# First layer of a three-layer attention kernel: the order of VectorE's work inside a softmax step, and who makes half of a low part

## The chip, the cores and the metric

One core of one Trainium2 chip. The metric is the device time of one launch, in microseconds (us). Engines as the profile names them: PE is TensorE, DVE is VectorE, ACT is ScalarE, POOL is GpSimd, SP is SyncE, which only issues the loads and stores here.

## The reference, cut to what matters

Sixteen sequences of 128 tokens, width 512. A grouped-query cross-attention layer (32 query heads of width 16, 8 key heads), a residual and a layer norm with scale and offset; then two cross-attention layers (16 heads of width 128, one extra key and value each) with a pre-norm, and an MLP of 2048. The change touches the first layer only:

```python
q = (x @ Wq + bq);  k = (ctx @ Wk + bk);  v = (ctx @ Wv + bv)      # per head
s = q @ k.T / 4 + mask
p = softmax(s)                       # max, exp, sum, reciprocal, product
o = (p @ v) @ Wo + bo + x
y = layernorm(o) * gamma + beta      # eps 1e-6
```

## The kernel before, in words

**Numbers in two parts.** Matrix operands of the projections are kept as a rounded part ("high") and the rest ("low", the value less its high part), and each product is three matrix products over them (`PASSES`, line 25). So every projected tile is evicted from PSUM twice: ScalarE writes the high part, then VectorE computes value less high part from the same PSUM bank. `qlo0` (line 1462) does so for the queries, `cxlo0` (line 1490) for the contexts, `klo0` (line 1453) for the keys. The four source tensors (`src_hi`, `src_lo`, numbers 0 to 3) get their high part from ScalarE (`high`, line 1146) and their low part from VectorE (`low`, line 1431) or GpSimd (`low`, line 448).

**Two halves.** The outer loop `hf` runs over two halves of eight sequences. In each, the first layer is 32 softmax steps (`STEPS0`); a step `s` is one sequence and eight heads. Four steps make a unit, and every unit has a projected query tile and gives a context tile. Every fourth to eighth step carries extra work: a query projection at the steps of `Q_AT` (line 45), an output product `out0` at those of `ROWS_AT` (line 52), a piece of a later weight split or an add of the output bias on GpSimd at those of `SPLIT_AT` and `BO_AT`.

**A step, engine by engine.** Each engine runs its own list in the order written, and waits on semaphores.

- TensorE, step `s` (line 834): transposes `t0(s)` (needs `norm0` of GpSimd), product with the values `pv0(s-1)`, scores `s0_(s+4)` (line 729; needs `z0` of the step before, since there is one set of score banks, and `q0_lo`), a query projection if `s` is in `Q_AT`, an output product `out0(s)` (line 770) if it is in `ROWS_AT`.
- VectorE, step `s` (line 1591): `rec0(s+1)` (a sum over three heads and a reciprocal), `cxlo0` if due, `qlo0` if due, `soft0(s+3)`, and the row work `add0` if due: it adds the output product to the residual `X` (line 1440).
- `soft0(s)` (line 1468) is two instructions: the masked copy (line 1473) reads the scores from PSUM, adds the mask, writes them to SBUF and raises `z0`; the maximum (line 1478) reads that copy, after a wait on `z0`, and raises `max0`.
- ScalarE, step `s` (line 1239): copies the transposes out of PSUM, evicts the high part of a query or context tile, then does the exponentials of step `s+3` (five heads with the maximum as bias, three heads after GpSimd's subtraction).
- GpSimd, step `s` (line 531): `norm(s+1)` (the product with the reciprocals, line 479), `sub(s+3)` (subtracts the maximum from three heads, line 472; needs `max0`), then the bias add or weight pieces.

**One bank, three users.** The query projection and `out0` write the same PSUM bank, `BA`. So `out0` waits for the low part of the last query that was projected there, and the next writer waits for the row work (`xadd`):

```python
def out0(s):                                                   # line 770
    pe.wait_ge(cx0_lo, u0 + (2 * n + 2))
    pe.wait_ge(q0_lo, u0 + 2 + sum(k < s for k in Q_AT))
    if n or t:
        pe.wait_ge(xadd, x0 + (n * BT + t))
```

`Q_AT` has the steps 0, 3, 8, 12, 16, 20, so `qlo0` runs on VectorE at steps 2, 5, 10, 14, 18, 22. `ROWS_AT` has 9, 10, 11, 13, 17, 18, 19, 21, 25, 26, 27, 28, so `add0` runs at 10, 11, 12, 14, 18, 19, 20, 22, 26, 27, 28, 29. Both fall on steps 10, 14, 18 and 22. `cxlo0` runs at steps 5, 9, 13, 17, 21, 25 and 29.

**The start of the first half.** VectorE makes both parts (two instructions) of the low part of source 3 between `soft0(2)` and the steps, line 1589. GpSimd's list there is `sub(0)`, `sub(1)`, `norm(0)`, `sub(2)` (line 527). In the second half that low part is made elsewhere (line 1575).

Of the kernel before, what the change touches and what calls it, by code (L numbers as in the profile page):

```python
# [17 lines left out]
F32 = mybir.dt.float32  # L18
F32R = mybir.dt.float32r
ALU = mybir.AluOpType  # L20
# [9 lines left out]
SEQ = 8  # L30
TB = 2
BT = SEQ // TB
# [12 lines left out]
Q_AT = {0: 2, 3: 3, 8: 4, 12: 5, 16: 6, 20: 7}  # L45
# [6 lines left out]
ROWS_AT = {9: (0, 0), 10: (0, 1), 11: (0, 2), 13: (0, 3), 17: (1, 0), 18: (1, 1), 19: (1, 2), 21: (1, 3),  # L52
           25: (2, 0), 26: (2, 1), 27: (2, 2), 28: (2, 3)}
# [24 lines left out]
def build(nc, x, xT, cT, mask, wq, wk0, wk, wv0, wv, wo, vec, ident_in, gb_rows, bo_rows, bv_rows, biasv_rows, out):  # L78
    ctx = ExitStack()
    with ctx:  # L80
# [3 lines left out]
        def sem(name):  # L84
            return ctx.enter_context(nc.semaphore(name))

        X = sb("X", [P, SEQ, D])
        at = (nc.sbuf_base + 31) // 32 * 32
# [29 lines left out]
        at = (nc.sbuf_base + 127) // 128 * 128  # L118
# [43 lines left out]
        BA, BB, BC, BD, BS, BPT, BPV = 0, 1, 2, 3, 4, 6, 7  # L162
# [15 lines left out]
        src_hi, src_lo = [sem(f"{k}_hi") for k in ("c0", "x0", "c1", "x1")], [sem(f"{k}_lo") for k in ("c0", "x0", "c1", "x1")]  # L178
# [15 lines left out]
        bo_tile, bo_added, vb_done, low_rows = sem("bo_tile"), sem("bo_added"), sem("vb_done"), sem("low_rows")  # L194
# [15 lines left out]
        def source(i, p, a):  # L210

            return (CT, AT)[i % 2][:, a, 2 * p:2 * p + 2, i // 2 * BTOK:(i // 2 + 1) * BTOK]

        def raw_source(i, p):

            return RAWS[i % 2][:, 1, 2 * p:2 * p + 2, i // 2 * BTOK:(i // 2 + 1) * BTOK]
# [10 lines left out]
        def jj0(u):  # L227

            return u // 4 * 2 + u % 2

        def tile0(s):

            return s // 8 % 2 * BT + s % 4
# [192 lines left out]
        def _(pool):  # L426
# [38 lines left out]
            for hf in range(HALVES):  # L465
                nq, nv = hf * Q_SLABS, hf * V_SLABS

                def sub(s):

                    pool.wait_ge(max0, hf * STEPS0 + (s + 1))  # L470
                    z = P0[s % BUFS0].rearrange("p (h t) -> p h t", t=P)[:, OWN:KV0, :]
                    nc.gpsimd.tensor_tensor(z, z, MX[:, s % BUFS0, OWN:KV0].unsqueeze(2).to_broadcast([P, KV0 - OWN, P]),  # L472
                                            ALU.add).then_inc(sub0, 1)

                def norm(s):

                    pool.wait_ge(rc0, hf * STEPS0 + (s + 1))
                    z = P0[s % BUFS0].rearrange("p (h t) -> p h t", t=P)
                    nc.gpsimd.tensor_tensor(z, z, RC[:, s % 2, :].unsqueeze(2).to_broadcast([P, KV0, P]),  # L479
                                            ALU.mult).then_inc(norm0, 1)  # L480
# [44 lines left out]
                    nc.gpsimd.tensor_tensor(BVR[:, 0:256], BVR[:, 0:256], ROWV[:, 0:256], ALU.subtract).then_inc(vb_done, 1)  # L525

                sub(0)
                sub(1)
                norm(0)
                sub(2)  # L530
                for s in range(STEPS0):
# [8 lines left out]
                    if s in SPLIT_AT:  # L540
                        n, parts = SPLIT_AT[s]
# [17 lines left out]
                for ly in range(LAYERS):  # L559
# [53 lines left out]
                    n = b0 + (NB1 - 1)  # L613
# [804 lines left out]
        def _(dve):  # L1418
            V_ = nc.vector
# [11 lines left out]
            def low(hf, i):  # L1431

                for p in range(2):
                    dve.wait_ge(src_hi[i], hf * 2 + (p + 1))
                    V_.tensor_tensor(source(i, p, 1), raw_source(i, p), source(i, p, 0).bitcast(F32),  # L1435
                                     ALU.subtract).then_inc(src_lo[i], 1)

            def add_rows(bank, tile, filled, count, done):
                dve.wait_ge(filled, count)
                V_.tensor_tensor(X[:, tile, :], PS[:, bank, :], X[:, tile, :], ALU.add).then_inc(done, 1)  # L1440
# [8 lines left out]
            for hf in range(HALVES):  # L1449
# [3 lines left out]
                def klo0(tb):  # L1453
                    dve.wait_ge(k0_hi, hf * TB + (tb + 1))
                    for e in range(2):
                        tiles = slice(tb * BT, (tb + 1) * BT)
                        ins = V_.scalar_tensor_tensor(KZ[:, 1, tiles, e, :], KF[:, tb, :].rearrange("p (b t) -> p b t", t=P),
                                                      VEC[:, COL_EVEN + e:COL_EVEN + e + 1], KZ[:, 0, tiles, e, :].bitcast(F32),
                                                      ALU.mult, ALU.subtract)
                    ins.then_inc(k0_lo, 1)  # L1460

                def qlo0(u):
                    jj = jj0(u)
                    dve.wait_ge(q0_hi, u0 + (u + 1))
                    V_.scalar_tensor_tensor(Q0[:, u % 2, 1, :], PS[:, BA, :], VEC[:, COL_BQ0 + jj:COL_BQ0 + jj + 1],  # L1465
                                            Q0[:, u % 2, 0, :].bitcast(F32), ALU.add, ALU.subtract).then_inc(q0_lo, 1)

                def soft0(s):
                    tile = tile0(s)
                    dve.wait_ge(s0_ps, s0 + (s + 1))  # L1470
                    if s >= BUFS0:
                        dve.wait_ge(t0_ps, s0 + (s - BUFS0 + 1))
                    V_.tensor_tensor(P0[s % BUFS0].rearrange("p (i e t) -> p i e t", e=2, t=P),
                                     PS[:, B0:B0 + 4, 0:256].rearrange("p i (e t) -> p i e t", t=P),
                                     BIASVR[:, tile * P:(tile + 1) * P].unsqueeze(1).unsqueeze(1).to_broadcast([P, 4, 2, P]),
                                     ALU.add).then_inc(z0, 1)
                    dve.wait_ge(z0, s0 + (s + 1))
                    V_.tensor_reduce(MX[:, s % BUFS0, :], P0[s % BUFS0].rearrange("p (h t) -> p h t", t=P),
                                     AXX, ALU.max, negate=True).then_inc(max0, 1)

                def rec0(s):
                    dve.wait_ge(exp0, s0 + (s + 1))
                    V_.tensor_reduce(SUM0[:, s % 2, OWN:KV0], P0[s % BUFS0].rearrange("p (h t) -> p h t", t=P)[:, OWN:KV0, :],
                                     AXX, ALU.add).then_inc(sum0, 1)
                    if s >= 2:
                        dve.wait_ge(norm0, s0 + (s - 1))
                    dve.wait_ge(sum0, s0 + (s + 1))
                    V_.reciprocal(RC[:, s % 2, :], SUM0[:, s % 2, :]).then_inc(rc0, 1)

                def cxlo0(u):  # L1490
                    dve.wait_ge(cx0_hi, u0 + (u + 1))
                    V_.scalar_tensor_tensor(CX0[:, u % 3, 1, :], PS[:, BB, :], VEC[:, COL_BV0:COL_BV0 + 1],
                                            CX0[:, u % 3, 0, :].bitcast(F32), ALU.add, ALU.subtract).then_inc(cx0_lo, 1)

                def add0(n, t, bank):
                    add_rows(bank, n % 2 * BT + t, o0_ps, o0 + (n * BT + t + 1), xadd)

                def stats(tb, tiles, added):

                    for i, b in enumerate(tiles):
                        dve.wait_ge(xadd, added + i)
                        V_.bn_stats(BNS[:, b, :], X[:, tb * BT + b, :]).then_inc(ln_stats, 1)
# [5 lines left out]
                def variances(r, eps):  # L1509

                    dve.wait_ge(ln_stats, r * BT + BT)
                    take_wait(dve)
                    for b in range(BT):
                        ins = V_.bn_aggr(MV[:, b, :], BNS[:, b, :])
                    step(r, 1, ins)
                    V_.tensor_scalar(NT[:], MV[:, :, 1], eps, -0.5, ALU.add, ALU.mult).then_inc(ln_step, 1)
# [63 lines left out]
                if hf:  # L1580
                    last_down((0, 1))
                qlo0(1)
                soft0(1)
                rec0(0)
                if hf:
                    last_down((2, 3))
                soft0(2)
                if hf == 0:
                    low(0, 3)
                x0 = hf * (ROWS0 + LAYERS * NB1 * BT)  # L1590
                for s in range(STEPS0):
                    if s + 1 < STEPS0:
                        rec0(s + 1)
                    if s % 4 == 1 and s > 1:
                        cxlo0(s // 4 - 1)
                    if s - 2 in Q_AT:
                        qlo0(Q_AT[s - 2])
                    if s + 3 < STEPS0:
                        soft0(s + 3)
                    if s == 0:  # L1600
                        klo0(1)
                    if s - 1 in ROWS_AT:
                        n, t = ROWS_AT[s - 1]
                        if n < 2:
                            dve.wait_ge(bo_tile, hf * SEQ + (n * BT + t + 1))
                        add0(n, t, BA)
                    if s == 29:
                        stats(0, range(BT), x0 + 9)
                        variances(hf * 8, 1e-6)
                    if s == 30:  # L1610
                        roots(hf * 8)
                        own(0, 0)
# [322 lines left out]
```

## Time and profile before

| | us |
|---|---|
| median of three runs (2405.12, 2407.29, 2408.05) | 2407.29 |
| the profiled execution, its own time | 2409.09 |
| its span, first to last instruction | 2407.0 |
| PE busy | 2347.7 |
| DVE busy | 1209.7 |
| ACT busy | 871.2 |
| POOL busy | 813.7 |

How to read it: the span is what the trace shows; the own time is 2.09 us more, which lies outside it. PE is busy almost throughout, but the first layer of each half is a short stage in which the four engines hand small tiles to one another, and the averages over the whole say little of it. Steps 0 to 31 of the first half lie between 33 us and 165 us of the span, those of the second half between 1227 us and 1360 us. In a row of the timeline the columns are: start, duration, engine, line, operation, what is written and read, shapes, count, and in brackets the idle time of that engine before it and who ended it. Idle of less than 0.15 us gets no brackets. MX is written by the maximum, XN, HF and P0D are the four buffers of masked scores (XN holds two), CX, Q and X are written by the context, query and row work.

### The profile page before, as it was taken

What the parts mean: (1) busy time and instruction counts of PE and PEld (TensorE: products, weight loads), DVE (VectorE), ACT (ScalarE), POOL (GpSimd) and SP (SyncE); (2) the same over time, 40 slices, a digit from 0 to 9 for tenths busy, and PEclk for the clock granted to TensorE, in tenths of its full rate; (3) what the DMA queues carried; (4) which work ended last, traced back from release to release, by engine and by line L of the source; (5) the groups of instructions that cost most, each with busy time, mean ns of one, the idle gap of its engine ahead of it and who ended that gap; (6) DMA issues with size and microseconds to landing.
All of it is one profiled execution on the core that took longest, in us unless ns stands there. A gap on an engine that the chain in (4) does not pass through costs nothing.

```text
span 2407.0 us, 35909 instructions
## 1 busy us (share of the span) xinstructions
PE 2347.7 (98%) x13616; PEld 1967.9 (82%) x13616; DVE 1209.7 (50%) x2037; ACT 871.2 (36%) x2511; POOL 813.7 (34%) x599
## 2 busy tenths in 40 slices
PE   7999999999999999999989999999999999999999
PEld 5677888888888888878867778888888888888887
DVE  6985333344533334465679843343354333344655
ACT  7964222232422222342378642222233222134311
POOL 6974323233422323120059543231343323132100
PEclk9999999999999999999999999999999999999999
DMA  5002111111101111211320021110111111110110
GB/s 207 12 19 84 36 36 52 44 62 58 36 25 46 35 44 44 66 44 62 112 86 11 19 83 36 44 61 27 62 58 36 36 36 35 44 53 14 62 44 35
DMA packets 37845, 120.54 MB, mean 50 GB/s; under 512 B 3664, under 2 KB 3920, under 8 KB 37712
## 3 DMA queue, kind: packets, MB, share of 16 engines
q1 hardware_dynamic: 37712, 118.69, 14.6%
q8 instruction: 93, 1.52, 0.3%
q14 instruction: 40, 0.33, 0.0%
HBM read 114.48 MB, written 4.19 MB: 49 GB/s over the span
## 4 chain that ended last, share of the span: by engine, by line
PE 85%; POOL 7%; DVE 4%; ACT 2%; issue 2%; DMA 0%; SPq 0%; POOLq 0%; DVEq 0%; ACTq 0%
PE PS L652 72%; PE PS L880 5%; PE PS L896 4%; PE PS L888 2%; POOL XN L479 1%; DVE X L1440 1%; POOL XN L472 1%; POOL W L503 1%; POOL HF L479 1%; ACT AT L1266 1%; POOL P0D L479 1%; POOL X L513 1%; ACT PS L1266 1%; POOL W L428 1%; PE PS L752 0%
## 5 line engine op out<-in xcount | busy, mean ns | idle before, releaser
L652 PE MATMUL PS<-AT,W 128*128 128x512 f32 x2496 | 605.4, 393 | 8.7 <-DVE AT L1561 5.4
L652 PEld LDWEIGHTS PS<-AT,W 128*128 128x128 f32 x2496 | 467.7, 189 | 113.8 <-DVE AT L1561 11.7
L1440 DVE TENSOR_TENSOR X<-PS,X 128x512 f32<-128x512 f32 x416 | 286.0, 689 | 359.4 <-PE PS L652 353.6
L550 POOL TENSOR_TENSOR PR<-PR,RC 128x512 f32<-128x512 f32 x128 | 133.4, 1042 | 926.4 <-DVE RC L1649 926.4
L652 PE MATMUL PS<-W,CX 128*128 128x512 f32 x1632 | 403.8, 398 | 6.9 <-DVE Q L1465 4.6
L652 PE MATMUL PS<-CT,W 128*128 128x512 f32 x1584 | 394.1, 398 | 7.7 <-DVE CT L1435 7.7
L652 PE MATMUL PS<-WV,CT 128*128 128x512 f32 (+1 forms) x1920 | 367.1, 349 | 0.0
L652 PEld LDWEIGHTS PS<-W,CX 128*128 128x128 f32 x1632 | 298.0, 188 | 72.5 <-issue 7.1
L652 PEld LDWEIGHTS PS<-WV,CT 128*128 128x128 f32 x1920 | 308.7, 189 | 45.5 <-issue 0.8
L652 PEld LDWEIGHTS PS<-CT,W 128*128 128x128 f32 x1584 | 289.5, 189 | 62.4 <-issue 7.9
L1293 ACT ACTIVATE CX<-PS,VEC 128x512 fp32r<-128x512 f32 x128 | 88.3, 690 | 648.2 <-PE PS L896 648.2
L1282 ACT ACTIVATE PR<-PS,MX 128x129 f32<-128x129 f32 x512 | 182.2, 370 | 177.5 <-DVE MX L1643 177.5
L1276 ACT ACTIVATE Q<-PS,BQS 128x512 f32<-128x512 f32 x128 | 88.2, 689 | 327.4 <-PE PS L652 327.4
L1688 DVE TENSOR_TENSOR VV<-PS,BVR 128x512 f32<-128x512 f32 x96 | 66.4, 692 | 258.4 <-PE PS L652 258.4
L428 POOL TENSOR_SCALAR W<-RAW 128x1024 fp32r<-128x1024 f32 (+2 forms) x107 | 96.2, 899 | 262.5 <-PE PS L652 214.2
L421 POOL TENSOR_TENSOR W<-RAW,W 128x1024 fp32r<-128x1024 f32 (+1 forms) x67 | 159.7, 2383 | 5.6
L1680 DVE SCALAR_TENSOR_TENSOR CX<-PS,VEC,CX 128x512 fp32r<-128x512 f32 x128 | 96.1, 751 | 129.2 <-ACT CX L1293 129.2
L880 PE MATMUL PS<-K,Q 128*128 128x129 f32 x1024 | 135.8, 276 | 0.9 <-ACT Q L1276 0.9
L1394 ACT ACTIVATE HF<-PS,VEC 128x512 f32<-128x512 f32 x64 | 44.0, 688 | 239.7 <-PE PS L652 239.7
L880 PEld LDWEIGHTS PS<-K,Q 128*128 128x128 f32 x1024 | 124.6, 192 | 1.6 <-ACT Q L1276 1.3
L1649 DVE RECIPROCAL RC<-SUM 128x4 f32<-128x4 f32 x128 | 22.7, 178 | 194.2 <-ACT PR L1282 194.2
L896 PEld LDWEIGHTS PS<-PT,VV 128*128 128x128 f32 x768 | 100.5, 191 | 7.5
(124 smaller groups left out, 2910.1 us busy)
## 6 DMA issues: line engine op xcount, KB each, us to landing
RAW<-in_wq SPq DMA_DIRECT2D x44, 512.0 KB, 4.3
RAW<-in_wo SPq DMA_DIRECT2D x44, 512.0 KB, 3.5
RAW<-in_wk SPq DMA_DIRECT2D x40, 512.0 KB, 3.5
RAW<-in_wv SPq DMA_DIRECT2D x40, 512.0 KB, 3.9
raw_c<-in_cT SPq DMA_DIRECT2D x8, 512.0 KB, 6.9
raw_x<-in_xT SPq DMA_DIRECT2D x8, 512.0 KB, 6.0
BVR<-in_bv_rows SPq DMA_DIRECT2D x8, 512.0 KB, 3.6
X<-in_x SPq DMA_DIRECT2D x4, 1024.0 KB, 10.8
```

The lines of the kernel that those rows point to most:

```text
L421: eng.tensor_tensor(SLAB[n][:, 1, 0:width], RAW[:, n, 0:width], SLAB[n][:, 0, 0:width].bitcast(F32), ALU.subtract).then_inc(w_ready[n], 1)
L428: return nc.gpsimd.tensor_scalar(out, in_, 1.0, 0.0, ALU.mult, ALU.add)
L479: nc.gpsimd.tensor_tensor(z, z, RC[:, s % 2, :].unsqueeze(2).to_broadcast([P, KV0, P]), ALU.mult).then_inc(norm0, 1)
L550: nc.gpsimd.tensor_tensor(PR[:, :, 0:P], PR[:, :, 0:P], RC[:, 0, 0:BT].unsqueeze(2).to_broadcast([P, BT, P]), ALU.mult).then_inc(norm_done, 1)
L652: ins = nc.tensor.matmul(out, lhs(c, a), rhs(c, b), start=(k == 0), stop=(k == total - 1))
L880: ins = nc.tensor.matmul(PS[:, BS + b // 2, b % 2 * 256:b % 2 * 256 + T1], Q[:, b * P:(b + 1) * P], K[:, h, b, 0:T1], start=True, stop=True)
L896: ins = nc.tensor.matmul(PS[:, BPV, b * P:(b + 1) * P], v[:, tb, b, col + h * P:col + (h + 1) * P], PT[:, b * P:(b + 1) * P], start=True, ...
L1276: nc.scalar.activation(Q[:], PS[:, BA, :], ACT.Identity, bias=BQS[:, bass.ds(ly * H1 + head, 1)], scale=K1 ** -0.5).then_inc(q_ev, 1)
L1282: ins = nc.scalar.activation(PR[:, b, 0:T1], PS[:, BS + b // 2, b % 2 * 256:b % 2 * 256 + T1], ACT.Exp, bias=MX[:, 0, b:b + 1], accum_out= ...
L1293: nc.scalar.activation(CX[:, tb, h, 0, :], PS[:, BPV, :], ACT.Identity, bias=VEC[:, bass.ds(cols + g * 2 + (COL_BIASV + h), 1)]).then_inc( ...
L1440: V_.tensor_tensor(X[:, tile, :], PS[:, bank, :], X[:, tile, :], ALU.add).then_inc(done, 1)
L1680: V_.scalar_tensor_tensor(CX[:, tb, h, 1, :], PS[:, BPV, :], VEC[:, bass.ds(cols + g * 2 + (COL_BIASV + h), 1)], CX[:, tb, h, 0, :].bitcas ...
```

## The change

In the first layer the context, query and row work that VectorE has in a step goes between the two instructions of that step's `soft0`. The context and query work stood before the masked copy, the row work behind the maximum. In the last steps (29 to 31), which have no `soft0`, the order stays. At the start of the first half the first of the two instructions of source 3's low part goes from VectorE to GpSimd, between `sub(0)` and `sub(1)`.

```diff
@@ GpSimd, start of a half
                 sub(0)
+                if hf == 0:
+                    low(3, 0)
                 sub(1)
@@ VectorE
-                def soft0(s):
+                def soft0(s, between=()):
                     tile = tile0(s)
                     dve.wait_ge(s0_ps, s0 + (s + 1))
...
                                      ALU.add).then_inc(z0, 1)
+                    if 'context' in between:
+                        cxlo0((s - 3) // 4 - 1)
+                    if 'query' in between:
+                        qlo0(Q_AT[s - 5])
+                    if 'row' in between:
+                        row0(s - 4)
                     dve.wait_ge(z0, s0 + (s + 1))
...
+                def row0(s):
+                    n, t = ROWS_AT[s]
+                    if n < 2:
+                        dve.wait_ge(bo_tile, hf * SEQ + (n * BT + t + 1))
+                    add0(n, t, BA)
...
                 soft0(2)
                 if hf == 0:
-                    low(0, 3)
+                    dve.wait_ge(src_hi[3], 2)
+                    V_.tensor_tensor(source(3, 1, 1), raw_source(3, 1), source(3, 1, 0).bitcast(F32),
+                                     ALU.subtract).then_inc(src_lo[3], 1)
                 for s in range(STEPS0):
                     if s + 1 < STEPS0:
                         rec0(s + 1)
-                    if s % 4 == 1 and s > 1:
-                        cxlo0(s // 4 - 1)
-                    if s - 2 in Q_AT:
-                        qlo0(Q_AT[s - 2])
                     if s + 3 < STEPS0:
-                        soft0(s + 3)
+                        soft0(s + 3, [k for k, at in (('context', s % 4 == 1 and s > 1), ('query', s - 2 in Q_AT), ('row', s - 1 in ROWS_AT)) if at])
+                    else:
+                        if s % 4 == 1:
+                            cxlo0(s // 4 - 1)
+                        if s - 1 in ROWS_AT:
+                            row0(s - 1)
                     if s == 0:
                         klo0(1)
-                    if s - 1 in ROWS_AT:
-                        n, t = ROWS_AT[s - 1]
-                        if n < 2:
-                            dve.wait_ge(bo_tile, hf * SEQ + (n * BT + t + 1))
-                        add0(n, t, BA)
```

## Rows read from the trace of the kernel before

**Rows 1.** The page, parts 1 and 4: busy times, and the chain by engine.

```profile
PE 2347.7 (98%) x13616; PEld 1967.9 (82%) x13616; DVE 1209.7 (50%) x2037; ACT 871.2 (36%) x2511; POOL 813.7 (34%) x599
PE 85%; POOL 7%; DVE 4%; ACT 2%; issue 2%; DMA 0%; SPq 0%; POOLq 0%; DVEq 0%; ACTq 0%
```

**Rows 2.** Busy times by stretch: steady steps of either half, first line the columns.

```profile
core 0: us, PE busy (x) PEld busy (x) DVE busy (x) ACT busy (x) POOL busy (x), PEclk, DMA share, GB/s
...
72.00:130.00 58.00, 53.06 (x605) 41.08 (x603) 54.60 (x75) 52.73 (x186) 57.34 (x55) 1.00 0.03 10
...
1250.00:1310.00 60.00, 52.38 (x612) 40.11 (x612) 53.86 (x72) 54.04 (x188) 57.17 (x54) 0.94 0.09 31
```

**Rows 3.** Timeline of POOL: the subtractions of steps 9 and 10, first half.

```profile
76.43 0.82 POOL L472 TENSOR_TENSOR XN<-XN,MX 128x384 f32<-128x384 f32 x1
...
80.32 0.82 POOL L472 TENSOR_TENSOR XN<-XN,MX 128x384 f32<-128x384 f32 x1
```

**Rows 4.** Timeline of POOL: where it waited for the maximum, both halves.

```profile
45.31 0.83 POOL L472 TENSOR_TENSOR XN<-XN,MX 128x384 f32<-128x384 f32 x1 [0.29 <-DVE MX L1478]
...
61.06 0.83 POOL L472 TENSOR_TENSOR XN<-XN,MX 128x384 f32<-128x384 f32 x1 [0.37 <-DVE MX L1478]
...
1254.92 0.83 POOL L472 TENSOR_TENSOR XN<-XN,MX 128x384 f32<-128x384 f32 x1 [1.61 <-DVE MX L1478]
```

**Rows 5.** Timeline of DVE: step 10 of the first half, query to row work.

```profile
75.68 0.70 DVE L1465 SCALAR_TENSOR_TENSOR Q<-PS,VEC,Q 128x512 fp32r<-128x512 f32 x1
76.30 1.21 DVE L1473 TENSOR_TENSOR XN<-PS,BIASVR 128x1024 f32<-128x1024 f32 x1
77.55 1.22 DVE L1478 TENSOR_REDUCE MX<-XN 128x8 f32<-128x1024 f32 x1
78.69 0.68 DVE L1440 TENSOR_TENSOR X<-PS,X 128x512 f32<-128x512 f32 x1
```

**Rows 6.** Timeline of PE: scores and output product of step 9, first half.

```profile
75.37 0.63 PE L740 MATMUL PS<-KZ,Q 32*128 32x256 f32 x12
76.53 1.62 PE L652 MATMUL PS<-W,CX 128*128 128x512 f32 x6 [0.53 <-DVE Q L1465]
```

**Rows 7.** DVE and POOL at steps 14, 18 and 22 of the first half.

```profile
92.35 1.22 DVE L1473 TENSOR_TENSOR XN<-PS,BIASVR 128x1024 f32<-128x1024 f32 x1
...
95.76 0.83 POOL L472 TENSOR_TENSOR XN<-XN,MX 128x384 f32<-128x384 f32 x1
...
107.14 0.70 DVE L1465 SCALAR_TENSOR_TENSOR Q<-PS,VEC,Q 128x512 fp32r<-128x512 f32 x1
...
111.20 0.85 POOL L472 TENSOR_TENSOR XN<-XN,MX 128x384 f32<-128x384 f32 x1
...
123.94 1.23 DVE L1473 TENSOR_TENSOR XN<-PS,BIASVR 128x1024 f32<-128x1024 f32 x1
...
129.08 0.82 POOL L472 TENSOR_TENSOR XN<-XN,MX 128x384 f32<-128x384 f32 x1
```

**Rows 8.** DVE and POOL at step 10 of the second half.

```profile
1271.70 1.23 DVE L1473 TENSOR_TENSOR XN<-PS,BIASVR 128x1024 f32<-128x1024 f32 x1 [0.55 <-PE PS L740]
...
1274.26 0.83 POOL L472 TENSOR_TENSOR XN<-XN,MX 128x384 f32<-128x384 f32 x1
```

**Rows 9.** The start of the first half: low parts on POOL and DVE.

```profile
21.92 4.78 POOL L450 TENSOR_TENSOR CT<-raw_c,CT 128x1024 fp32r<-128x1024 f32 x2 [4.83 <-ACT CT L1150]
...
30.78 0.83 POOL L472 TENSOR_TENSOR XN<-XN,MX 128x384 f32<-128x384 f32 x1 [3.29 <-DVE MX L1478]
...
34.17 2.98 DVE L1435 TENSOR_TENSOR AT<-raw_x,AT 128x1024 fp32r<-128x1024 f32 x2
...
40.11 1.98 DVE L1457 SCALAR_TENSOR_TENSOR KZ<-KF,VEC,KZ 128x512 fp32r<-128x512 f32 x2
```

**Rows 10.** Timeline of DVE: context work of step 5, first half.

```profile
57.19 0.75 DVE L1492 SCALAR_TENSOR_TENSOR CX<-PS,VEC,CX 128x512 fp32r<-128x512 f32 x1 [1.14 <-ACT CX L1198]
```

**Rows 11.** Timeline of PE: last output product of the steps, first half.

```profile
151.38 1.61 PE L652 MATMUL PS<-W,CX 128*128 128x512 f32 x6 [0.20 <-DVE X L1440]
```

## The prediction

> **What bounds the kernel now.** I read the busy times first: TensorE is busy for 98% of the span and makes 85% of the chain that ended last, and GpSimd, which is busy for only a third of the span, makes 7% of that chain [rows 1]. The reader is to see that mismatch: an engine that idles on the whole binds somewhere. The second view, busy time by stretch, says where. In the steady steps of the first layer GpSimd is busy 57.3 of 58 us in the first half, and 57.2 of 60 us in the second, more than any other engine [rows 2]. The third view is its timeline: from one subtraction to the next it takes 80.32 - 76.43 = 3.89 us and never waits [rows 3]. Among all its rows from 43 to 155 us only two show a wait, 0.29 and 0.37 us [rows 4]. So in the first layer GpSimd sets the pace, and what follows that layer depends on its result and runs on a full TensorE. Time lost or won by GpSimd in these 2 x 32 steps therefore moves the end by as much. VectorE's own time counts only where its maximum comes later than GpSimd wants it.
>
> **Part 1, context and query work behind the masked copy.** The instructions and their number stay, the maximum still comes behind the same work, and so the order alone is no loss where nothing waits. What can be won is the wait for ScalarE's high part: at step 5 VectorE sat idle 1.14 us for the context [rows 10], and the copy, 1.21 us [rows 5], fits into that wait. GpSimd waited there for 0.37 us in the first half and 1.61 us in the second [rows 4], which caps the gain. In the first half I take all 0.37. In the second I take 0.6 between the bounds of 0 and 1.21 (the copy's length), for the copy can't start before TensorE has the scores. At the other context steps GpSimd has no wait in the first half, so nothing is won.
>
> A second gain could come from the pair itself. The maximum starts 1.25 us after the copy, 0.04 behind its end, while the copy starts 0.62 us after the query work of 0.70, 0.08 ahead of its end [rows 5]: work that doesn't read what was just written starts 0.12 us earlier. There are 18 steps in a half with work in between, at most 2.2 us of VectorE's time in a half, all of it beside GpSimd's, and I cost it at nothing. The Trainium skill speaks against that gain (VectorE: DVE Perf Modes, "The DRAIN you can't avoid": the next instruction waits until the pipe is empty, and a semaphore adds nothing). By that rule it is nothing on VectorE too; the rows differ from it by 0.12 us, and the sum is the same by either.
>
> **Part 2, row work ahead of the maximum.** A maximum comes 0.6 us later. Where no query work is in the step, the lead covers it: at step 11 and its like the output product is nearly done when the copy ends. I cost seven such steps in each half at nothing. If their cover were gone, each would cost up to 0.6 us.
>
> **Part 3, query and row work in one step.** This is where I see the cost. At steps 10, 14, 18 and 22 both are due, and they are tied: the output product that the row work adds can't start before the query's low part is read out of bank BA, and TensorE indeed waited 0.53 us for exactly that [rows 6]. Before the change copy and maximum stood between the two, 78.69 - 76.30 = 2.4 us, and the product of 1.62 us ran beside them [rows 5, 6]. After it VectorE does copy, query work, then stands still for the whole product, then row work, and only then the maximum. Everything behind the waiting instruction on VectorE is held too, the next reciprocal among it, and the maximum is what GpSimd's subtraction and ScalarE's exponentials need. TensorE starts the product later as well, with the next transposes behind it.
>
> From the start T of the copy: 1.12 us to the query work (the copy's 1.21 less about 0.09), 0.85 from its start to the product's (75.68 to 76.53), 1.62 for the product, 0.05 to see it, 0.60 for the row work (0.68 less 0.08), 1.22 for the maximum, 0.08 to GpSimd: T + 5.54 us [rows 5, 6]. The 0.05 and 0.08 are estimates from the 0.04 above.
>
> - Step 10: the scores end at 75.37 + 0.63 = 76.00 [rows 6], so T is 76.05, and the subtraction can start at 81.59 instead of 80.32 [rows 3]: +1.3.
> - Step 14: the copy at 92.35 stays where TensorE lets it; 97.89 instead of 95.76 [rows 7]: +2.1.
> - Step 18: the copy takes the place of the query work at 107.14; 112.68 instead of 111.20: +1.5.
> - Step 22: 123.94 gives 129.48 instead of 129.08: +0.4. GpSimd has two weight pieces in each of the two steps before, so it comes late there.
>
> That is 5.3 us in the first half. In the second, step 10 has a later copy, T = 1271.70, and a subtraction at 1274.26 [rows 8]: 1277.24, +3.0. From there GpSimd is as late against TensorE as in the first half, and I take the same 2.1, 1.5 and 0.4: 7.0 us. The bounds of this part are 0, if VectorE had caught up each time, and 17.3 us, if every collision of the second half cost 3.0.
>
> **Part 4, the low part.** The instruction that goes to GpSimd takes 4.78 / 2 = 2.39 us there and falls into an idle stretch of 3.29 us [rows 9]; it is cost at nothing, and if that cover were gone it would cost 2.4. VectorE is freed of 2.98 / 2 = 1.49 us. Little of it arrives: the keys' low part at 40.11 waits for ScalarE anyway and the next reciprocal is behind it [rows 9], so what remains is GpSimd's wait of 0.29 before 45.31 [rows 4]. Between 0 and 0.29 I take 0.1.
>
> **The end of the steps.** TensorE's last output product waited 0.20 us for the row work [rows 11], which now comes ahead of the maximum; 0.2 us in either half. No DMA is issued or moved, and SP's queue isn't touched.
>
> **The sum.** 5.3 + 7.0 = 12.3 lost; 0.37 + 0.6 + 0.1 + 0.4 = 1.5 won; net +10.8 us. On the profiled execution's own time, 2409.1, that is 2419.9. That execution is 1.8 above the median of the three runs, so against the median, 2407.3, it is **2418.1 us**. Two tenths of a per cent, about what a measurement of this kernel can tell from no change, is 4.8 us here.
>
> **Rivals.**
>
> *Absorbed.* VectorE and TensorE catch up between collisions, and only part of the 12.3 us reaches GpSimd. For it: VectorE is busy 54.6 of 58 us [rows 2], so it has 3.4 us of slack, and the pairs save up to 2.2. Against it: GpSimd has only 0.7 us, and it can't catch up. A third of the loss, less the gains, is +2.6: 2409.9, not told from no change.
>
> *Faster.* The copy hides in the waits for ScalarE at all seven context steps, the scores are released earlier, and TensorE has the product ready when VectorE asks for it. Its place is step 10; it decides if the product could start before the query's low part, that is, if the wait on `q0_lo` were met by an earlier query. Then all of GpSimd's waits, 0.29 + 0.37 + 1.61, go, and with 1.5 from the low part and 0.4 at the end it is -4.2 or, with the smaller waits that have no row here, about -5: 2402. Against it stands TensorE's wait of 0.53 us on that very low part [rows 6].
>
> **How the numbers follow.** The forecast has 0.70, the low clock 0.14, absorbed 0.11, faster 0.05. So slower by over 0.2% is 0.84, within it 0.11, faster 0.05. The forecast's own spread is 2413 to 2421: it is lower if steps 18 and 22 cost nothing in both halves and higher if step 14 costs 3.0. The range takes in the low clock up to 2423 and reaches down to 2410.5, into the absorbed case; faster is left out.
>
> **What would show it.** In the new profile GpSimd's subtractions of steps 10, 14 and 18 carry waits of 1.3 to 3 us for the maximum, in both halves; VectorE's row work in these steps has an idle of about 1.8 us for TensorE's product; TensorE waits longer for the query's low part. The wait of 0.37 at step 5 is gone, the low part on GpSimd ends before its second subtraction, and the stage behind the steps is as long as it was. The prediction is wrong if these subtractions still follow without a wait, or if they wait and the steps are made up for afterwards.

## The result, and the profile after

| | before | after |
|---|---|---|
| median on one chip, four runs each | 2407.40 us | 2422.02 us |
| lowest to highest | 2405.12 to 2408.05 | 2420.2 to 2422.53 |
| profiled execution, own time | 2409.09 | 2420.2 |
| its span | 2407.0 | 2418.2 |

The change makes the kernel slower: the ratio is 1.0062, 95% interval 1.0047 to 1.0076, and the medians differ by 14.6 us. The forecast had 10.8 us; its sign and its range held, its size was 3.8 us short. The two profiled executions differ by only 11.1 us. Most of what is missing there lies at the start of the kernel: the subtraction at 45.31 us [rows 4] comes at 42.76 in the new profile, 2.55 us earlier, and 1.80 of that is already there when GpSimd's first low part starts (20.12 us instead of 21.92 [rows 9]), ahead of every instruction that the change touches. Over the fourteen profiled executions that start lies between 18.44 us (e7) and 22.82 us (e10). So stages are compared below, and not spans.

The busy times first, as in [rows 1]. TensorE is busy for as long (2348.3 for 2347.7 us) in a longer span, so what is added is waiting:

```profile
PE 2348.3 (97%) x13616; PEld 1968.1 (81%) x13616; DVE 1205.7 (50%) x2036; ACT 871.0 (36%) x2511; POOL 815.1 (34%) x600
```

The busy times of the two steady stretches, columns as in [rows 2], show where. In the same 58 and 60 us GpSimd, which set the pace, is busy 48.85 and 53.88 us instead of 57.34 and 57.17. The granted clock has gone from 1.00 and 0.94 to 0.91 in both:

```profile
72.00:130.00 58.00, 50.36 (x538) 38.59 (x530) 44.70 (x62) 45.38 (x154) 48.85 (x45) 0.91 0.01 1
1250.00:1310.00 60.00, 51.75 (x576) 39.45 (x568) 50.45 (x70) 51.95 (x178) 53.88 (x52) 0.91 0.11 37
```

GpSimd's timeline, all its waits for the maximum from 50 us to the end of the steps in the first half, and from 1250 us on in the second. They answer to [rows 3], [rows 4], [rows 7] and [rows 8]:

```profile
79.50 0.83 POOL L472 TENSOR_TENSOR XN<-XN,MX 128x384 f32<-128x384 f32 x1 [2.13 <-DVE MX L1487]
83.90 0.83 POOL L472 TENSOR_TENSOR HF<-HF,MX 128x384 f32<-128x384 f32 x1 [0.45 <-DVE MX L1487]
98.33 0.83 POOL L472 TENSOR_TENSOR XN<-XN,MX 128x384 f32<-128x384 f32 x1 [2.84 <-DVE MX L1487]
102.45 0.83 POOL L472 TENSOR_TENSOR HF<-HF,MX 128x384 f32<-128x384 f32 x1 [0.24 <-DVE MX L1487]
116.31 0.83 POOL L472 TENSOR_TENSOR XN<-XN,MX 128x384 f32<-128x384 f32 x1 [2.22 <-DVE MX L1487]
121.00 0.83 POOL L472 TENSOR_TENSOR HF<-HF,MX 128x384 f32<-128x384 f32 x1 [0.77 <-DVE MX L1487]
135.41 0.83 POOL L472 TENSOR_TENSOR XN<-XN,MX 128x384 f32<-128x384 f32 x1 [0.41 <-DVE MX L1487]
...
1280.61 0.83 POOL L472 TENSOR_TENSOR XN<-XN,MX 128x384 f32<-128x384 f32 x1 [1.97 <-DVE MX L1487]
1285.17 0.83 POOL L472 TENSOR_TENSOR HF<-HF,MX 128x384 f32<-128x384 f32 x1 [0.62 <-DVE MX L1487]
1299.55 0.83 POOL L472 TENSOR_TENSOR XN<-XN,MX 128x384 f32<-128x384 f32 x1 [2.78 <-DVE MX L1487]
1316.48 0.83 POOL L472 TENSOR_TENSOR XN<-XN,MX 128x384 f32<-128x384 f32 x1 [1.47 <-DVE MX L1487]
1335.26 0.83 POOL L472 TENSOR_TENSOR XN<-XN,MX 128x384 f32<-128x384 f32 x1 [0.92 <-DVE MX L1487]
```

Two kinds of wait stand there. The four large ones of a half belong to steps 10, 14, 18 and 22: 7.60 us in the first half, 7.14 in the second. The small ones directly behind them (0.45, 0.24, 0.77, 0.62; 2.08 us) belong to steps 11, 15 and 19. The waits of 0.37 and 1.61 us at step 5 [rows 4] are gone. The second half of before had two more, of 0.15 and 0.32 us, at steps 11 and 13. The balance of the waits is 14.7 + 2.1 - 2.5 = 14.4 us.

The timeline agrees. From the subtraction at 45.31 us [rows 4] to the last product with the reciprocals, GpSimd takes 112.7 us before and 121.6 after (to 157.99 and 164.33 us); in the second half, from 1237.93 and 1244.03 us, it takes 114.7 and 120.2 (to 1352.66 and 1364.18 us). That is 8.9 + 5.4 = 14.3 us more, about the loss, and next to nothing is made up for later.

Step 10 on VectorE, beside [rows 5]: copy, query, the stand-still of 2.68 us, row, maximum:

```profile
73.04 1.23 DVE L1476 TENSOR_TENSOR XN<-PS,BIASVR 128x1024 f32<-128x1024 f32 x1 [1.06 <-PE PS L742]
74.18 0.74 DVE L1467 SCALAR_TENSOR_TENSOR Q<-PS,VEC,Q 128x512 fp32r<-128x512 f32 x1
77.60 0.69 DVE L1442 TENSOR_TENSOR X<-PS,X 128x512 f32<-128x512 f32 x1 [2.68 <-PE PS L654]
78.21 1.21 DVE L1487 TENSOR_REDUCE MX<-XN 128x8 f32<-128x1024 f32 x1
...
82.01 0.69 DVE L1442 TENSOR_TENSOR X<-PS,X 128x512 f32<-128x512 f32 x1 [0.41 <-PE PS L654]
```

And on TensorE, beside [rows 6]. It waits 2.08 us for the query's low part instead of 0.53, and what it does next is slow: the output product takes 2.42 us instead of 1.62, and eight transposes take 1.89 us. Three steps on, eight of them take 1.04 us (third row). The last two rows are step 14 of the second half:

```profile
75.07 2.42 PE L654 MATMUL PS<-W,CX 128*128 128x512 f32 x6 [2.08 <-DVE Q L1467]
77.29 1.89 PE L754 MATMUL PS<-IDENT,HF 128*128 128x128 f32 x8
...
90.29 1.04 PE L754 MATMUL PS<-IDENT,XN 128*128 128x128 f32 x8
...
94.65 1.68 PE L654 MATMUL PS<-W,CX 128*128 128x512 f32 x6 [2.19 <-DVE Q L1467]
96.12 1.91 PE L754 MATMUL PS<-IDENT,HF 128*128 128x128 f32 x8
...
112.21 2.09 PE L654 MATMUL PS<-W,CX 128*128 128x512 f32 x6 [2.19 <-DVE Q L1467]
114.10 1.91 PE L754 MATMUL PS<-IDENT,HF 128*128 128x128 f32 x8
...
131.78 1.63 PE L654 MATMUL PS<-W,CX 128*128 128x512 f32 x6 [2.19 <-DVE Q L1467]
133.24 1.04 PE L754 MATMUL PS<-IDENT,HF 128*128 128x128 f32 x8
...
1295.91 1.63 PE L654 MATMUL PS<-W,CX 128*128 128x512 f32 x6 [2.19 <-DVE Q L1467]
1297.38 1.03 PE L754 MATMUL PS<-IDENT,HF 128*128 128x128 f32 x8
```

The busy times of three short stretches behind the new idle, of steps 10, 14 and 22, give the granted clock there (0.59, 0.72, 1.00):

```profile
75.00:79.20 4.20, 4.13 (x18) 3.27 (x22) 1.60 (x2) 0.25 (x1) 2.37 (x2) 0.59 0.00 0
...
94.60:98.00 3.40, 3.35 (x18) 2.73 (x20) 1.57 (x2) 0.12 (x1) 0.89 (x1) 0.72 0.03 5
...
131.70:135.00 3.30, 3.22 (x34) 2.57 (x38) 1.49 (x2) 0.83 (x2) 3.21 (x4) 1.00 0.00 0
```

So at steps 10 and 14, and by the durations at 18, the new idle is followed by work mostly at the lower of TensorE's two levels, 1.2 GHz. At step 22 it is not. In the second half it is so at steps 10 and 22 (products of 2.25 and 2.27 us, transposes of 1.91), and not at 14 and 18 (1.63 and 1.03 us at both). So the work is slow behind five of the eight idles. All four small waits of GpSimd stand behind such a slow stretch, and none behind the other steps. The forecast's sum had every product at 1.62 us.

### The profile page after: what moved, and what is told of

It is laid out like the page before. It is cut to its first block, busy times and chain, and to the rows that moved or that the text cites. A ratio compares the mean times of both kernels' runs of the same rounds, so it can differ in the third digit from the quotient of the medians.

```text
span 2418.2 us, 35909 instructions
## 1 busy us (share of the span) xinstructions
PE 2348.3 (97%) x13616; PEld 1968.1 (81%) x13616; DVE 1205.7 (50%) x2036; ACT 871.0 (36%) x2511; POOL 815.1 (34%) x600
## 3 DMA queue, kind: packets, MB, share of 16 engines
q1 hardware_dynamic: 37712, 118.69, 14.7%
## 4 chain that ended last, share of the span: by engine, by line
PE 87%; POOL 4%; DVE 4%; ACT 2%; issue 1%; DMA 0%; SPq 0%; POOLq 0%; DVEq 0%; ACTq 0%
PE PS L654 73%; PE PS L882 5%; PE PS L898 4%; PE PS L890 2%; PE PS L754 1%; PE PS L767 1%; POOL W L503 1%; POOL XN L479 1%; ACT AT L1268 1%; DVE X L1442 1%; ACT PS L1268 1%; PE PS L742 1%; POOL HF L479 1%; POOL P0D L479 0%; POOL W L428 0%
## 5 line engine op out<-in xcount | busy, mean ns | idle before, releaser
L654 PEld LDWEIGHTS PS<-W,CX 128*128 128x128 f32 x1632 | 299.2, 189 | 85.5 <-issue 20.2
L1662 DVE RECIPROCAL RC<-SUM 128x4 f32<-128x4 f32 x128 | 22.7, 178 | 194.2 <-ACT PR L1284 194.2
## 6 DMA issues: line engine op xcount, KB each, us to landing
X<-in_x SPq DMA_DIRECT2D x4, 1024.0 KB, 10.8
```

The costliest lines, as they stand in the source:

```text
L654: ins = nc.tensor.matmul(out, lhs(c, a), rhs(c, b), start=(k == 0), stop=(k == total - 1))
```

## The experiments

Twelve kernels, each timed in five rounds against the kernel before on the same chip (4 to 6 executions of e1, e6, e8 and e10, 11 of the others; the groups named under the table ran on three chips). In the short diffs `due` is what the step has to do, `inside` what goes between copy and maximum; the rest keeps its place of before (context and query ahead of the copy, row behind the maximum).

| kernel | us | against before |
|---|---|---|
| e1_pairs_only | 2427.07 | 1.0088 [1.0072, 1.0103] |
| e2_pairs_back | 2404.88 | 0.9992 [0.9983, 1.0001] |
| e3_low_alone | 2405.10 | 0.9995 [0.9986, 1.0004] |
| e4_context_only | 2402.34 | 0.9983 [0.9974, 0.9992] |
| e5_query_first | 2406.28 | 0.9997 [0.9988, 1.0006] |
| e6_row_behind | 2423.17 | 1.0062 [1.0048, 1.0076] |
| e7_one_pair | 2411.52 | 1.0025 [1.0016, 1.0034] |
| e8_fill | 2417.55 | 1.0046 [1.0032, 1.0060] |
| e9_best | 2403.99 | 0.9987 [0.9978, 0.9996] |
| e10_behind_fill | 2415.27 | 1.0030 [1.0018, 1.0042] |
| e11_before_fill | 2409.80 | 1.0013 [1.0004, 1.0022] |
| e12_context_alone | 2404.34 | 0.9991 [0.9982, 1.0000] |

The kernel before had a median of 2406.87 us beside e1 to e4, 2407.06 beside e5, e6, e8 and e9, 2406.81 beside e10 to e12, and 2406.41 beside e7.

**Where is the loss: the four steps with both, or the rest?**

```diff
-soft0(s + 3, due)
+inside = due if 'query' in due and 'row' in due else []        # e1
+inside = [] if 'query' in due and 'row' in due else due        # e2
+soft0(s + 3, inside)                     # low part as before, in both
```

> The order of the kernel before, except in steps 10, 14, 18 and 22, where query and row work both go between copy and maximum. Theory (VectorE stands still for the output product that its own query work has just released): the whole loss is here, 2419 to 2423 us, and GpSimd's subtractions of steps 10, 14 and 18 wait 1.5 to 3 us for the maximum. Rival (every later maximum and every later query part costs a little, in all 18 steps with work between): 4 of 18 steps, so about 2410 us.

> The new order in all steps except 10, 14, 18 and 22, which keep the order before; the low part is made as before. Theory: nothing is left of the loss, 2405 to 2408 us, and only the subtraction of step 5 comes earlier (0.37 and 1.61 us of GpSimd's waits gone). Rival (18 steps share the loss): about 2418 us.

The four steps alone cost 20.2 us, more than the whole change and than I expected. All the rest together is 2.0 us faster, an interval that just reaches no change. In e2 the wait at step 5 was to go in both halves; in the second it is still 1.07 us. GpSimd's timeline in e1 has the waits at the same four steps, and at step 10 4.33 us instead of 2.13:

```profile
80.91 0.82 POOL L472 TENSOR_TENSOR XN<-XN,MX 128x384 f32<-128x384 f32 x1 [4.33 <-DVE MX L1485]
...
100.02 0.83 POOL L472 TENSOR_TENSOR XN<-XN,MX 128x384 f32<-128x384 f32 x1 [3.63 <-DVE MX L1485]
```

So the place of the loss is shown. The two parts don't add up to the whole: 20.2 - 2.0 = 18.2 against 14.6. Why e1's waits are longer is settled in part only. The work is slow behind six of its eight idles, and the eight products take 5.0 us more than 8 x 1.62, where those of the change take 2.6 more. At step 10 of the first half that is 2.90 us instead of 2.42, 0.5 of the 2.2.

**One pair instead of four.**

```diff
+inside = due if s == 14 else []          # low part as before
```

> The order of before everywhere, low part as before, and only at step 14 the query and the row work between copy and maximum: one pair in each half instead of four. If every pair costs by itself, this is a quarter of e1's 20.2 us, about 5: 2411 to 2413, with a wait of some 2 us for the maximum at step 14 in either half, and the lower clock on the next transposes. If the pairs cost only together (each one late finds the step before it late), it is 2407 to 2409. My sum priced this step at 2.1 us a half, 4.2 in all, 2411.

It cost 5.1 us. GpSimd's timeline has one new wait for it in each half, 2.65 and 2.64 us, which is 5.3 us (step 5, in the order of before, waits 1.68 and 0.34 us here where it waited 0.37 and 1.61, the same in sum); TensorE's shows the 2.19 us of idle and 1.91 for the transposes behind it:

```profile
95.86 0.83 POOL L472 TENSOR_TENSOR XN<-XN,MX 128x384 f32<-128x384 f32 x1 [2.65 <-DVE MX L1485]
...
1291.08 0.83 POOL L472 TENSOR_TENSOR XN<-XN,MX 128x384 f32<-128x384 f32 x1 [2.64 <-DVE MX L1485]
```

```profile
91.94 1.91 PE L652 MATMUL PS<-W,CX 128*128 128x512 f32 x6 [2.19 <-DVE Q L1465]
93.65 1.91 PE L752 MATMUL PS<-IDENT,HF 128*128 128x128 f32 x8
```

So a pair costs by itself, and a wait at GpSimd arrives at the end in full. My 2.1 us for this step were 0.55 short; the product was 0.29 us slower than 1.62 (0.55 in the second half).

**Which of the two moves: the query or the row?** Context work and the shared low part are as in the change.

```diff
+inside = [k for k in due if k != 'query']                      # e5
+inside = [k for k in due if not (k == 'row' and 'query' in due)]  # e6
```

> As the change, but the query work goes back ahead of the copy; context and row work stay between copy and maximum. Theory: the output product then runs beside the copy, VectorE waits for it some 0.8 us instead of 2 to 2.7, and the maximum of steps 14 and 18 is late by about 0.4 us only: 2404 to 2407 us. Rival (it is the row work ahead of the maximum that costs, whatever stands before it): 2415 us or more.

> As the change, but in steps 10, 14, 18 and 22 the row work goes back behind the maximum; the query work stays between copy and maximum. Theory: the maximum is on time, but the output product still starts 1.2 us late with TensorE idle for 2 us ahead of it, and VectorE waits about 1 us for it with the next reciprocal behind: 3 to 8 us more than before, 2410 to 2415 us. Rival (only the maximum matters, and it is on time): 2404 to 2407 us.

This is where my explanation fell. With the row between and the query ahead, the time is that of before (-0.8 us). With the query between and the row behind the maximum, where I expected most of the loss back, the whole of it stays: +16.1.

The row isn't free either. The kernel e9, further down, ran on the same chip and differs from e5 only in that the row of these four steps stands behind the maximum. It takes 2403.99 us, so the row ahead of the maximum costs 2.3 us. GpSimd's timeline in e5 has these waits at steps 10 and 14, and two more of 0.26 and 0.70 us in the second half, 2.4 us in all:

```profile
79.38 0.83 POOL L472 TENSOR_TENSOR XN<-XN,MX 128x384 f32<-128x384 f32 x1 [0.86 <-DVE MX L1487]
...
95.47 0.83 POOL L472 TENSOR_TENSOR XN<-XN,MX 128x384 f32<-128x384 f32 x1 [0.60 <-DVE MX L1487]
```

From e9 to e6 only the query's place differs, and that is 19.2 us. (e5 and e9 have the queries of steps 2 and 5 ahead of the copy too; e1 shows that the loss needs only the four steps.) VectorE and GpSimd at step 10 of e6, in two timelines:

```profile
75.08 1.23 DVE L1476 TENSOR_TENSOR XN<-PS,BIASVR 128x1024 f32<-128x1024 f32 x1 [1.35 <-PE PS L742]
76.22 0.74 DVE L1467 SCALAR_TENSOR_TENSOR Q<-PS,VEC,Q 128x512 fp32r<-128x512 f32 x1
76.88 1.21 DVE L1487 TENSOR_REDUCE MX<-XN 128x8 f32<-128x1024 f32 x1
80.12 0.69 DVE L1442 TENSOR_TENSOR X<-PS,X 128x512 f32<-128x512 f32 x1 [2.02 <-PE PS L654]
```

```profile
78.17 0.83 POOL L472 TENSOR_TENSOR XN<-XN,MX 128x384 f32<-128x384 f32 x1 [0.65 <-DVE MX L1487]
...
81.66 1.90 POOL L479 TENSOR_TENSOR XN<-XN,RC 128x1024 f32<-128x1024 f32 x1 [1.43 <-DVE RC L1503]
85.86 0.83 POOL L472 TENSOR_TENSOR HF<-HF,MX 128x384 f32<-128x384 f32 x1 [2.31 <-DVE MX L1487]
```

The maximum is nearly in time (0.65 us late). But VectorE still stands still for the product, 2.02 us, now with the next reciprocal behind it, and GpSimd waits for that and then for the next maximum. The lateness comes from the query's low part: behind the copy it releases the product late. Once the product is late, the row's place only decides at which of GpSimd's waits it appears: the change (+14.6) and e6 (+16.1) can't be told apart, the more so as the executions of e6 lie between 2417.92 and 2426.28 us, and the profile shows the slowest of them. In e5 TensorE has its scores at 75.17 and its product at 75.72, with no wait, and the row waits 0.42 us.

**How much is the lower clock?** Twelve matrix products whose result nobody reads go ahead of TensorE's wait for the low part, into a bank that is free then: into the change (e8), into e6 (e10) and into the kernel before (e11).

```diff
 n, t = ROWS_AT[s]
+if s - 1 in Q_AT:
+    pe.wait_ge(t0_ev, s0 + (s + 1))
+    for _ in range(12):
+        nc.tensor.matmul(PS[:, BPT, 0:256], CT[:, 0, 0, 0:P],
+                         CT[:, 0, 0, 0:256], start=True, stop=True)
 pe.wait_ge(cx0_lo, u0 + (2 * n + 2))
```

> The changed kernel with 12 products of 256 columns more on TensorE ahead of the wait of each output product of steps 9, 13, 17 and 21, into a bank that is free there; their result is overwritten. They only keep TensorE busy in the 2.1 us for which it waits for the query's low part. Theory (half of the loss is the wait itself, the rest the lower clock that it brings on, at which the output product takes 1.7 to 2.4 us and the transposes 1.9 instead of 1.0): the granted clock stays up there, 8 times about 0.8 to 1 us come back, 2413 to 2416 us. Rival (the clock costs nothing, since GpSimd and VectorE wait anyway): 2422 us or a little more.

> The order of e6 (row work behind the maximum in steps 10, 14, 18 and 22) with the twelve filler matrix products of e8 ahead of TensorE's wait for the query's low part, which fill most of its 2.1 us there. The idle and the clock are told apart. If the loss of e6 (+16.1 us) is the lower clock alone, this is within 2 us of the kernel before. If it is the late low part, which the filler does not make earlier, about the same 4.5 us come back as in e8: 2416 to 2420. GpSimd's waits for the reciprocal at steps 10, 14 and 18 would then be there but shorter.

> A control: the kernel before, with the same filler products in the same four steps of either half. There TensorE waits only 0.5 us for the low part, so the filler should cost more than it fills: 0 to 5 us slower than before, with the granted clock near 1.00. If it is faster than before, the filler gives something of its own and e8 and e10 overstate what the clock took.

TensorE's timeline of e8 at step 10 and GpSimd's at steps 10, 14 and 18:

```profile
74.17 1.69 PE L777 MATMUL PS<-CT 128*128 128x256 f32 x12
76.26 1.62 PE L654 MATMUL PS<-W,CX 128*128 128x512 f32 x6 [0.41 <-DVE Q L1471]
77.72 1.03 PE L754 MATMUL PS<-IDENT,HF 128*128 128x128 f32 x8
```

```profile
79.88 0.83 POOL L472 TENSOR_TENSOR XN<-XN,MX 128x384 f32<-128x384 f32 x1 [1.35 <-DVE MX L1491]
...
97.84 0.83 POOL L472 TENSOR_TENSOR XN<-XN,MX 128x384 f32<-128x384 f32 x1 [2.48 <-DVE MX L1491]
...
114.78 0.83 POOL L472 TENSOR_TENSOR XN<-XN,MX 128x384 f32<-128x384 f32 x1 [1.49 <-DVE MX L1491]
```

The granted clock of the steady stretch of the first half is back at 1.00 (0.97 in the second), and at all eight steps the product takes 1.61 to 1.63 us and the transposes 1.03 or 1.04. The loss shrinks from 14.6 to 10.5 us; I had expected 2413 to 2416. The waits at the four steps are 1.35, 2.48, 1.49 and none in the first half, where the sum had 1.3, 2.1, 1.5 and 0.4, and 1.38, 2.46, 2.91 and none in the second, where it had 3.0, 2.1, 1.5 and 0.4. The small waits behind them are gone. In e10 the loss shrinks from 16.1 to 8.5, a little more than expected.

In the kernel before, where TensorE waits 0.53 us or less at six of the eight steps, the filler costs 3.0 us: the product follows it without a wait. In e8 it fits: each of the eight products still waits 0.40 to 0.54 us for the low part behind the filler, so it delays none of them. The clock's share of the change is therefore 4.1 us by the medians and 4.7 by GpSimd's waits at and behind the four steps (16.8 us after, 12.1 in e8). The intervals of the two kernels overlap (1.0047 to 1.0076, 1.0032 to 1.0060), so the size is rough. The larger part is the late low part itself.

**What do the other parts bring?**

```diff
-soft0(s + 3, due)
+inside = []                                        # e3
+inside = [k for k in due if k == 'context']        # e4, e12
+inside = [k for k in due if k == 'context' or (k == 'row' and 'query' not in due)]  # e9
```

e12 has the low part as before, the others have it shared with GpSimd.

> The order of the kernel before in every step; only the first half of source 3's low part goes to GpSimd. Theory (the keys' low part waits for ScalarE and nearly all is lost there): 0.1 to 0.3 us less, about 2407 us, no change that a measurement tells. Rival (the 1.5 us that VectorE saves arrive): 2405.9 us, with the stage of the first half 1.5 us shorter.

> Only the context work goes between copy and maximum, query and row work stay where they were before, and the low part is shared as in the change. Theory: the waits for ScalarE's high part are filled with the copy, GpSimd's waits at step 5 go: 1 to 2.5 us less than before, 2405 to 2406.5 us. Rival (the scores aren't there when the wait begins, so the copy only moves the wait): 2407 us, no change.

> Context work between copy and maximum, row work there too where the step has no query work, query work ahead of the copy, the low part shared as in the change. Theory: the gain of the context work (about 4 us) and 0.2 us at the end of either half's steps: 2402 us. Rival (row work ahead of the maximum brings nothing or takes 0.3 us where the product isn't done): the same as with the context work alone, 2402.3 us, or up to 2404.

> The kernel before with the context work behind the masked copy, all else as before (no shared low part). If the gain of e4 (-4.2 us) is the context's, this gives 2402 to 2404 beside 2407; if it needed the low part too, it is at 2405 to 2407. GpSimd's wait at step 5 (0.37 and 1.61 us) should be gone in both halves.

The low part alone: -1.8 us with an interval that reaches no change. From GpSimd's first low part to the subtraction at 45.31 us [rows 4] it is 23.4 us before and 23.0 us in the other five kernels without the sharing; with it, it is 22.6 to 22.7 us in seven and 23.0 in e4. So the sharing is worth some 0.3 us. VectorE's freed time is seen to end in a wait for ScalarE in the profile of the change too, beside [rows 9], and GpSimd then waits 2.05 us for the reciprocal:

```profile
26.31 2.40 POOL L450 TENSOR_TENSOR AT<-raw_x,AT 128x1024 fp32r<-128x1024 f32 x1
28.67 0.82 POOL L472 TENSOR_TENSOR XN<-XN,MX 128x384 f32<-128x384 f32 x1
...
40.38 1.90 POOL L479 TENSOR_TENSOR HF<-HF,RC 128x1024 f32<-128x1024 f32 x1 [2.05 <-DVE RC L1503]
```

```profile
37.65 1.88 DVE L1459 SCALAR_TENSOR_TENSOR KZ<-KF,VEC,KZ 128x512 fp32r<-128x512 f32 x2 [1.44 <-ACT KZ L1161]
```

Context work behind the copy with the low part is the fastest of all, 2402.34 us, 0.17% below the kernel before (interval 0.08 to 0.26%); without the low part it is 2404.34, with the rows added 2403.99. These three can't be told apart: their intervals overlap. Measured as above, from the subtraction at 45.31 us to the end of the steps and likewise in the second half, the two stages take 227.4 us before and 224.4, 225.5 and 225.3 in these three, so there is a gain of 1.9 to 3.0 us in the profiles.

How much of it is the order is less sure, for the wait at step 5 changes from kernel to kernel. Summed over both halves it is 1.98, 2.05, 2.02, 0.80 and 0.72 us in the five kernels with the context in the old place (before, e3, e7, e11, e1). In the nine with the context between it is 0 (the change and e4), 0.35 (e12), 0.42 (e5), 0.80 (e9), 1.04 (e10), 1.07 (e2), 2.02 (e6) and 2.09 (e8). The means are 1.5 and 0.9 us. In e12 I had expected it gone in both halves; in the first 0.35 us stayed.

## Why the prediction was right or wrong

**What bounds.** Right. GpSimd's waits rose by 14.4 us, its two stages by 14.3 and the time by 14.6; e7 repeats it with 5.3 and 5.1.

**Part 1.** Right in kind. The context at step 5 no longer waits ahead of the copy (VectorE has copy, context, query and maximum at 54.04, 55.18, 55.84 and 56.50 us, with no gap), against [rows 10]. I took 0.37 and 0.6 us; 0.37 and 1.61 went, 1.0 us more. That all of it went is luck: in e8, with the same order on VectorE, this wait is 1.05 and 1.04 us, and over all kernels the order is worth about 0.6 us in place of my 0.97. That independent work starts ahead of the copy's end holds in the new order too: the query part starts 1.14 us after a copy of 1.23 (step 10 above), 0.09 ahead of its end. It moved nothing that could be told.

**Part 2, row work at no cost.** Right for steps with nothing late before them (e9, where these rows are between, is not slower). Wrong directly behind a late pair: the row of step 11 waits 0.41 us for its product ahead of the maximum (82.01 above), as does that of step 19. The small waits of steps 11, 15 and 19 sum to 2.1 us, a term that the forecast put at nothing; step 15 has no row, so there it is only the lateness of step 14 that is left. They stand behind slow stretches alone and are gone in e8, so they are the clock's as well. My line that the cover holds looked at the old timeline, where the step before was in time.

**Part 3, the collision.** Place and sign right, size short. The table has GpSimd's wait as forecast and as measured, and the output product that the sum had at 1.62 us:

| step | forecast, us | measured, us | product, us |
|---|---|---|---|
| 10, first half | 1.3 | 2.13 | 2.42 |
| 14 | 2.1 | 2.84 | 1.68 |
| 18 | 1.5 | 2.22 | 2.09 |
| 22 | 0.4 | 0.41 | 1.63 |
| 10, second half | 3.0 | 1.97 | 2.25 |
| 14 | 2.1 | 2.78 | 1.63 |
| 18 | 1.5 | 1.47 | 1.63 |
| 22 | 0.4 | 0.92 | 2.27 |
| sum | 12.3 | 14.7 | |

**The term that was sized wrong most is the 1.62 us for the product in the chain T + 5.54 us**: that is the product at the higher clock level. The step that makes TensorE idle for 2.1 us also lowers its clock behind it, and the eight products took 2.6 us more in all. With the 2.1 us of small waits that makes 4.7, what e8 gives back. I had the low clock as a rival at 0.14 and priced it as two or three stretches of 1.7 us; it was no rival but a part of the forecast's own mechanism. That the clock is a smaller part than the late product is shown by e8 and e10, where 10.5 and 8.5 us of loss stay with every product near 1.62 us.

The clock doesn't explain all of the table. At step 14 of the second half everything ran at the higher level, and still the wait was 2.78 us for 2.1: the chain was T + 5.77 us, mostly since the product started 2.13 us after the copy instead of 1.97, and GpSimd came 2.99 us after the copy instead of 3.41. At step 10 of the second half it was the other way: GpSimd came 4.32 us after the copy instead of 2.56. In e1, where the steps ahead of it keep the order of before, this step has the 3.0 us that I took from [rows 8]. That the second half's total is near the forecast (7.14 for 7.0, and 6.75 in e8) is luck: its terms miss both ways.

The story around the sum was also put in the wrong place. I saw the trouble in the row work ahead of the maximum. e5, e6 and e9 show that the row there costs 2.3 us with the query ahead of the copy, and that the query behind the copy costs 19.2. The prediction's own sentence, that TensorE starts the product later, with the next transposes behind it, was the cause, and I treated it as the smaller half.

**Part 4.** Right: the low part of 2.40 us fits into the idle on GpSimd, and most of VectorE's freed time is lost in the keys' wait. Alone it is -1.8 us, within what can't be told from no change; the traces give some 0.3 us for my 0.1.

**The end of the steps.** The wait of [rows 11] is gone; its 0.2 us a half are too small to be seen.

**The other rivals.** Absorbed: refuted, the waits arrive in full (e7, and the two stages of the change). Faster: refuted; the product could not start before the query's low part (2.08 to 2.36 us of wait).

## What to carry to other kernels

When an instruction is moved a little later on an engine with slack, ask what it releases, not only what stands behind it: here a low part 1.1 us later let a third engine idle and cost 19.2 us, while the place of the row behind it cost 2.3. Price the released work at the clock that it will have after the new idle, and price the neighbours of a late step with their cover gone. A 2 x 2 of the moves (both in the change, one each in e5 and e6, neither in e9) costs little and finds the guilty one where the timeline points at its neighbour. And compare stages of a trace, not spans, where the start varies (by up to 4.4 us here, more than most of the smaller effects above).

## What the runs showed of the hardware that I had not expected

An idle of 2.1 us on TensorE was enough to have the next 2 to 3 us at the lower level: transposes of 1.03 us took 1.91, a product of 1.62 took up to 2.90. It is not certain each time: in the four traces that have such idles (the change, e1, e6, e7) there are 26, of 2.07 to 2.47 us, and 20 have slow work behind them. Behind 2.19 us at step 22 the same work took 1.63 and 1.04. The Trainium skill (TensorE: Matmul & The Clock Gate, "Part 1: The HAM clock gate") says that an idle array falls back to the lower clock; the rows of steps 10, 14 and 18 of the first half agree, those of step 22 there and of step 14 in the second half show that one such idle need not do it.

Keeping TensorE busy with products that nobody reads bought back 4.1 us and 7.6 us (e8, e10) in the two orders that made it idle, and lost 3.0 us in the one that didn't (e11).
